# Cross attention on one core: the queries of two row tiles made by one set of split products, and what is moved for it

## The chip, the core and the metric

One core of a Trainium2 chip runs the whole kernel in one launch. The metric is device time in microseconds. The kernel before has a median of 1503.9 us over three runs (1502.83 to 1505.37). TensorE (PE), VectorE (DVE), ScalarE (ACT), GpSimd (POOL) and SyncE (SP, which only issues DMAs here) each work through a queue of their own, and meet at semaphores. TensorE writes to PSUM, which has eight banks of 512 fp32 columns; DVE and ACT read it.

## The reference, cut to what matters

x is 64 sequences of 32 rows with 512 channels; the context is 64 sequences of 257 rows with 256 channels. Three layers follow each other, each with a residual: cross attention, a small self attention, and a mixture of experts (8 experts, 2 per row). The change is in the first:

```
Q = layernorm(x) @ Wq.T                         # 2048 x 512, 16 heads of 32
K, V = split(ctx @ Wkv.T)                       # 64 x 257 x 512 each
attn = softmax(Q K.T * 32**-0.5)                # per sequence and head: 32 x 257
x = x + (attn @ V) @ Wo.T
```

## The kernel before, in words

The 2048 rows are 16 tiles of 128 rows, that is four sequences each. Cross attention never makes K and V: a tile's queries are multiplied into Wk once (`absorb_k`, which makes `QK`, for all 16 heads), and the scores of a sequence are `QK` times the turned context. The weighted sum is taken over the raw context (`gather_z`) and goes through the value weights afterwards (`values`). So a tile has a part of its own (normalise, turn, project to queries, absorb, values, output projection) and four steps, one for each sequence, numbered s = 4i + j for tile i and sequence j: 64 steps.

A step has a fixed order on PE: `scores(s)` (24 products of 258 columns into the four banks of `bank_s`), `gather_z(s-1)` (12 products of 512 columns into `bank_u`), `turn_z(s+1)` (4 transposes of the next sequence's context), then what the tile's own part puts into this step, then `turn_p(s)` (8 transposes of the normalised probabilities into two banks of `bank_s`). In between DVE takes the maxima of the scores (L696), ACT the exponentials (L596), DVE the reciprocals and the division `Pr` (L703 to L708); then DVE subtracts the low part of the next `QK` (L633, `qk_lo`) and of the next turned context (L628, `z_lo`), for which ACT has made the high parts (L558 `qk_hi`, L541 `z_hi`). `scores(s+1)` waits for `z_lo(s+1)` (semaphore `v_T`). After `turn_p`, ACT and DVE copy and split the turned probabilities (L564, L641), which free the two banks for the next scores.

Numbers go as a high and a low part in fp32r: `product` (L49) issues three matmuls for each pair of operands (high by high, low by high, high by low; L52, L53, L54). The query projection is the exception: `project_q` (L394) multiplies plain fp32, `WqT` by the turned rows `xnT`, 128 columns a matmul, one tile at a time; its 16 matmuls of a tile show as 32 records.

What the tile's own part puts into the four steps of tile i: j=0: `turn_last`, `last_values` and `values` of tile i-1 (their result goes over `bank_o`); j=1: `project_o(i-1)` (12 products of 512 columns); j=2: `turn_x(i+2)` (L147, 4 transposes into `bank_o`, copied to `xnT` by ACT, L152) and the first half of `project_q(i+2)`; j=3: its second half. In j=0 and j=2 two `absorb_k` of the next tile (32 small matmuls, L404) stand ahead of them; ACT copies their result to `QK` (L551, two copies of 128x1024), and `turn_p` waits for that copy, because both use `bank_s`. `bank_o` is one bank: turned rows, queries, values and output projection take it in turn, each waiting until the one before has been read.

The order is written out by hand in `tile(i, u, first, last, more)` of each engine. `by_pair` runs tiles in pairs (u = 0 is the even tile, u = 1 the odd); the first and the last pair are written out, the six between are a loop. `more` is false in the last pair. Before it stands a setup block which loads and turns the weights, ending at a barrier, and then a short head which makes the first tiles' queries. The loads of the self attention's weights are issued by SP in the first tile (`weights.load`), and ACT waits for them behind the last step.

Of the kernel before, what the change touches and what calls it, by code (L numbers as in the profile page):

```python
# [23 lines left out]
P = 128  # L24
# [60 lines left out]
def cross_attention(nc, x_in, ctx_in, Wq, Wkv, Wo, x_res, ident, vlast_dram, spare,  # L85
# [21 lines left out]
    with ExitStack() as ctx:  # L107
# [6 lines left out]
        WqT = sb("WqT", [P, KC, C])  # L114
# [11 lines left out]
        key_of = sb("key_of", [P, HD], F32R)  # L126
        xn, xnT = spare_x[:, 0, :], spare_x[:, 1, :].rearrange("p (k q) -> p k q", q=P)
# [9 lines left out]
        pe_X, a_X = sem("pe_X"), sem("a_X")  # L137
# [12 lines left out]
        def x_out(act, i):  # L150
            act.wait_ge(pe_X, i + 1)
            act.copy(xnT.rearrange("p k q -> p (k q)"), bank_o[:]).then_inc(a_X, 1)  # L152

        def rows_of(i):


            return x_res[:, i % n_tile if isinstance(i, int) else i, :]
# [26 lines left out]
        with ExitStack() as setup:  # L184
# [12 lines left out]
            masked = setup.enter_context(nc.semaphore("w_masked"))  # L197
            own_key = sbs("own_key", [P, HD])
# [13 lines left out]
            for k in range(KC):  # L212
                jobs.append((0, [raw_q[:, o, k * P:(k + 1) * P] for o in range(KC)], (WqT[:, k, :], None), P))

            with nc.Block() as block:
# [26 lines left out]
                def _(pe):  # L242
# [4 lines left out]
                    for n, (load, blocks, _dst, width) in enumerate(jobs):  # L247
# [10 lines left out]
                        mm.then_inc(turned, 1)  # L258
                        if n == n_values - 1:
                            turn_x(pe, 0)  # L260

                @block.scalar
                def _(act):
                    for n, (_load, blocks, (hi, _lo), width) in enumerate(jobs):
                        act.wait_ge(turned, n + 1)
                        act.copy(hi, ring[n % 6][:, 0:len(blocks) * width]).then_inc(hi_done, 1)
                        if n == n_values - 1:
                            x_out(act, 0)

                @block.vector  # L270
                def _(dve):
# [3 lines left out]
                    for n, (_load, blocks, (hi, lo), width) in enumerate(jobs[:n_split]):  # L275
# [3 lines left out]
                    dve.tensor_reduce(own_key[:], ident[:].rearrange("p (h t) -> p t h", t=HD), AX_X, ALU.add  # L279
                                      ).then_inc(masked, 1)  # L280
                    dve.tensor_reduce(head_mask[:], ident[:].rearrange("p (h t) -> p h t", t=HD), AX_X, ALU.add
                                      ).then_inc(masked, 1)
                    for j in range(BT):
                        dve.tensor_reduce(row_mask[:].rearrange("p (m j) -> p m j", j=BT)[:, :, j],
                                          ident[:].rearrange("p (b j m) -> p j m b", j=BT, m=NQ)[:, j], AX_X, ALU.add
                                          ).then_inc(masked, 1)
                    dve.wait_ge(masked, 2 + BT)
                    dve.tensor_copy(key_of[:], own_key[:]).then_inc(masked, 1)
# [7 lines left out]
        QK = [sb(f"QK{u}", [P, KL, NH, P]) for u in range(2)]  # L296
# [42 lines left out]
        def step_of(i, u, j, more):  # L339

            if j % 2 == 0 and (more or u == 0):
                return 1 - u, j, 2 * (i + 1) + 2, BT * i + NQ + j + 2
            return None

        with nc.Block() as block:
            @block.sync
            def _(sp):
# [9 lines left out]
                def tile(i, u, first, last, more):  # L359
# [13 lines left out]
                    if first:  # L373
                        weights.load(sp)
                by_pair(sp, tile)

            @block.tensor
            def _(pe):
# [9 lines left out]
                def project_q(i, half, wait_first=True):  # L388
                    pe.wait_ge(a_X, i + 1)
                    if half == 1 and wait_first:  # L390
                        pe.wait_ge(a_Q, 2 * i + 1)
# [81 lines left out]
                project_q(0, 1, False)  # L473
                turn_z(0, 0, 0)
                pe.wait_ge(a_Q, 2)
                turn_x(pe, 1)
                absorb_k(Qp[0], 0)
                absorb_k(Qp[0], 1)
                project_q(1, 0)
# [4 lines left out]
                project_q(1, 1, False)  # L484
# [4 lines left out]
                pe.wait_ge(d_QK, NQ)  # L489

                def tile(i, u, first, last, more):
                    for j in range(BT):
# [3 lines left out]
                        scores(s, some)  # L496
                        if j == 0 and not first:
                            pe.wait_ge(a_Q, 2 * min(i + 2, n_tile) if isinstance(i, int) else 2 * i + 4)
# [39 lines left out]
            def _(act):  # L538
# [4 lines left out]
                def q_out(i, slot, halves):  # L543
                    act.wait_ge(pe_Q, 2 * i + max(halves) + 1)
# [1878 lines left out]
```

## Time and profile before

The profiled execution took 1500.6 us, 3.3 us less than the median; its span is 1498.8 us.

| | |
|---|---|
| median of three runs | 1503.9 us |
| profiled execution, its span | 1500.6 us, 1498.8 us |
| setup block | 0 to 19.1 us |
| cross attention, its 64 steps and their tail | 32.4 to 688 us |
| self attention, routing and experts | from 688 us |
| PE, DVE, ACT, POOL busy over the span | 96%, 73%, 54%, 36% |
| granted TensorE clock, mean | 0.988 of 2.4 GHz |

In a timeline row the first number is the start in us from the span's start, the second the length; a merged row has a count. In brackets stands how long the engine was idle before it and who released it. The ends of matmul records are modelled, so that consecutive records overlap; the distance between two starts is the time that PE spent.

### The profile page before, as it was taken

The page shows a single profiled execution, that of the slowest core. Times are in us where ns is not written, and L with a number is a line of the kernel's source. Part 1 is how long each engine was busy: PE and PEld are TensorE (multiplying, and loading weights), DVE is VectorE, ACT ScalarE, POOL GpSimd, SP SyncE. Part 2 cuts the span into 40 slices and gives each one's busy share as a digit, 9 for nine tenths or more (in the row PEclk, how much of TensorE's full clock was granted, in tenths as well). Part 3 has the DMA queues.
Part 4 walks back from the last instruction along what each step waited for, and adds up shares of the span by engine and source line. Part 5 has one row for each costly group of instructions (what it writes and reads, how often), then busy time and mean ns, then how long its engine had stood idle before and what let it go on. Part 6 is the DMA issues. An engine that isn't in the chain of part 4 may idle for free. (4 is left out here: it accounts for less than half of the span.)

```text
span 1498.8 us, 39481 instructions
## 1 busy us (share of the span) xinstructions
PE 1436.7 (96%) x14944; PEld 1284.1 (86%) x14944; DVE 1087.7 (73%) x1941; ACT 807.3 (54%) x1525; POOL 544.1 (36%) x814
## 2 busy tenths in 40 slices
PE   7999999999999999998899998799999999999998
PEld 6888888888888888876788787688999999999997
DVE  3677777777677776775567686797887878787885
ACT  4666666666666666654333434345555555555452
POOL 1222222222222222234866877453332333334232
PEclk9999999999999999999999999799999999999999
DMA  6301101100001100100001104179877878787871
GB/s 238 126 26 30 30 22 28 28 23 27 28 22 28 28 28 22 30 9 1 31 31 38 38 31 156 59 216 317 270 262 256 274 252 268 261 279 244 289 255 46
DMA packets 130733, 174.10 MB, mean 116 GB/s; under 512 B 16953, under 2 KB 89337, under 8 KB 130626
## 3 DMA queue, kind: packets, MB, share of 16 engines
q1 hardware_dynamic: 120242, 145.56, 30.1%
q0 software_dynamic: 10384, 27.05, 5.0%
q8 instruction: 74, 1.21, 0.3%
q14 instruction: 33, 0.27, 0.1%
HBM read 157.18 MB, written 19.06 MB: 118 GB/s over the span
## 5 line engine op out<-in xcount | busy, mean ns | idle before, releaser
L2215 DVE TENSOR_TENSOR split<-raw,split 128x1024 fp32r<-128x1024 f32 x204 | 242.3, 1220 | 6.6 <-ACT split L2155 4.0
L52 PE MATMUL bank<-split_xT,split 128*128 128x256 f32 x768 | 217.1, 283 | 0.4
L54 PE MATMUL bank<-split_xT,split 128*128 128x256 f32 x768 | 216.2, 282 | 0.0
L53 PE MATMUL bank<-split_xT,split 128*128 128x256 f32 x768 | 216.1, 281 | 0.0
L2155 ACT CAST split<-raw 128x1024 fp32r<-128x1024 f32 x202 | 203.2, 1048 | 5.9 <-DMA raw<-in_L_ffn_W_dram 4.0
L596 ACT ACTIVATE Pr<-xa_s,nmax 128x257 f32<-128x257 f32 x256 | 118.7, 473 | 125.1 <-DVE nmax L696 125.1
L2175 ACT ACTIVATE sl<-bank 128x256 f32<-128x256 f32 x115 | 44.2, 384 | 241.8 <-PE bank L54 232.8
L52 PE MATMUL xa_s<-split,split 128*128 128x258 f32 x512 | 150.6, 294 | 1.9 <-DVE split L628 1.9
L52 PEld LDWEIGHTS bank<-split_xT,split 128*128 128x128 f32 x768 | 145.5, 189 | 6.6 <-issue 2.5
L53 PEld LDWEIGHTS bank<-split_xT,split 128*128 128x128 f32 x768 | 145.6, 190 | 3.2
L53 PE MATMUL xa_s<-split,split 128*128 128x258 f32 x512 | 145.8, 285 | 0.0
L54 PEld LDWEIGHTS bank<-split_xT,split 128*128 128x128 f32 x768 | 145.4, 189 | 0.0
L54 PE MATMUL xa_s<-split,split 128*128 128x258 f32 x512 | 145.3, 284 | 0.0
L641 DVE TENSOR_TENSOR split<-xa_s,split 128x512 fp32r<-128x512 f32 x128 | 82.6, 686 | 81.4 <-ACT split L564 80.2
L2299 POOL TENSOR_TENSOR e_carrier<-count 128x1 f32<-128x1 f32 x84 | 27.2, 324 | 310.2 <-DMA of_row<-slot_val 106.2
L748 POOL TENSOR_TENSOR xa_carrier<-mhalf 128x1 f32<-128x1 f32 x64 | 12.6, 197 | 285.2 <-DVE split L633 280.6
L696 DVE TENSOR_REDUCE nmax<-xa_s 128x2 f32<-128x514 f32 x128 | 87.9, 690 | 33.2 <-PE xa_s L54 32.3
L52 PE MATMUL xa_u<-split,split_xT 128*128 128x512 f32 x256 | 102.3, 400 | 0.8 <-issue 0.8
L52 PE MATMUL bank<-split,a_hi 128*128 128x512 f32 x234 | 96.3, 411 | 7.0 <-DVE a_lo L2274 6.9
L52 PEld LDWEIGHTS xa_s<-split,split 128*128 128x128 f32 x512 | 98.1, 192 | 3.6 <-DVE split L628 2.6
L53 PE MATMUL xa_u<-split,split_xT 128*128 128x512 f32 x256 | 101.0, 395 | 0.0
L54 PE MATMUL xa_u<-split,split_xT 128*128 128x512 f32 x256 | 100.9, 394 | 0.0
(314 smaller groups left out, 3918.5 us busy)
## 6 DMA issues: line engine op xcount, KB each, us to landing
raw<-in_L_ffn_W_dram SPq DMA_DIRECT2D x207, 512.0 KB
raw<-in_ctx_dram SPq DMA_DIRECT2D x64, 256.0 KB, 2.6
out_dram<-x_res SPq DMA_DIRECT2D x16, 256.0 KB
xs<-xn SPq DMA_DIRECT2D x16, 256.0 KB
x_res<-in_x_dram SPq DMA_DIRECT2D x1, 3584.0 KB, 19.0
VL<-v_last_rows SPq DMA_DIRECT2D x128, 2.0 KB, 1.5
raw_o<-in_L_xattn_Wo_dram SPq DMA_DIRECT2D x1, 1024.0 KB, 6.5
raw_q<-in_L_xattn_Wq_dram SPq DMA_DIRECT2D x1, 1024.0 KB, 9.6
```

Of the source, the lines that this page charges most:

```text
L52: pe.matmul(out, lh, rh, start=start, stop=False)
L53: pe.matmul(out, ll, rh, start=False, stop=False)
L54: return pe.matmul(out, lh, rl, start=False, stop=stop)
L596: act.activation(Pr[:, m, 0:NK], bank_s[:, m, 0:NK], ACT.Exp, bias=nmax[:, m:m + 1], scale=1.0, accum_out=rsum[:, m:m + 1]).then_inc(a_E, 1)
L641: dve.tensor_tensor(PT_lo[:, c, :], bank_pt[c], PT_hi[:, c, :].bitcast(F32), ALU.subtract).then_inc(v_PT, 1)
L696: dve.tensor_reduce(nmax[:, 2 * h:2 * h + 2], bank_s[:, 2 * h:2 * h + 2, 0:NK], AX_X, ALU.max, negate=True).then_inc(v_mx, 1)
L748: pool.tensor_tensor(carrier[:], mhalf[:], mhalf[:], ALU.add)
L2155: aW.done(act.copy(hi, raw), f"p{c}{q}")
L2175: aM.done(act.activation(sl[:, j % 2, :], bank_hg[j % 2][:, 0:ROWS], ACT.Silu), f"{pos}s{j}")
L2215: vW.done(dve.tensor_tensor(lo, raw, hi.bitcast(F32), ALU.subtract), f"p{c}{q}")
L2299: pool.tensor_tensor(carrier[:], count[:, 0:1], count[:, 0:1], ALU.add).then_inc(carried, 1)
```

## The change

Only cross attention and its buffers change.

1. `project_q(i, half)` now makes the queries of tiles i and i+1 together, for even i. Operands are split: `WqT_hi`, `WqT_lo`, and `xT_hi`, `xT_lo` which hold the turned rows of two tiles side by side, 256 columns. A half is two blocks of 128 output channels by four of input channels by three matmuls: 24 matmuls of 256 columns, in j=2 and j=3 of the even tile; the odd tile has none. `q_out` writes a half for both tiles with one ACT instruction of 512 columns.
2. `x_out` makes two ACT copies of the turned rows (the plain one stays, and one into `xT_hi`), and a new `x_lo` on DVE subtracts into `xT_lo` (semaphore `v_X`).
3. The rows of tile i+3 are turned in tile i. In the even tile that is in j=2, straight behind the scores, ahead of `gather_z`; its `x_out` stands ahead of `qk_hi` on ACT, its `x_lo` ahead of `qk_lo` on DVE, and `normalise` has moved to the end of j=1. In the odd tile it is in j=3, ahead of `turn_z`; `x_out` stands there ahead of `z_hi`, `x_lo` behind `z_lo`. Tile 2 is turned in the second step of tile 0. `turn_last` in j=0 waits for `a_X`, `v_X` in even tiles and for `a_Q` in odd ones.
4. The odd tile's `project_o(i-1)`, and its `add_residual`, stand in j=2 instead of j=1.
5. Setup: the rows of tiles 0 and 1 are both turned and split there, `WqT` is split (four more DVE subtractions), and the masks (seven small DVE instructions) move behind the barrier. In the head one `project_q(0, half)` of 24 products stands for each half, the second behind the first pair of `absorb_k`.
6. The second `QK` buffer now lies over the places of the self attention's `wq` and `wo`. These two loads (1 MB each) are issued behind the last `qk_lo` (`v_QK`) instead of in the first tile; the others stay.

```diff
-        WqT = sb("WqT", [P, KC, C])
+        WqT_hi, WqT_lo = sb("WqT_hi", [P, KC, C], F32R), sb("WqT_lo", [P, KC, C], F32R)
+        xT_hi, xT_lo = sb("xT_hi", [P, KC, 2 * P], F32R), sb("xT_lo", [P, KC, 2 * P], F32R)
...
-        def x_out(act, i):
+        def x_out(act, i, slot):
             act.wait_ge(pe_X, i + 1)
-            act.copy(xnT.rearrange("p k q -> p (k q)"), bank_o[:]).then_inc(a_X, 1)
+            act.copy(xnT.rearrange("p k q -> p (k q)"), bank_o[:])
+            act.copy(xT_hi[:, :, slot * P:(slot + 1) * P], bank_o[:].rearrange("p (k q) -> p k q", q=P)).then_inc(a_X, 1)
+
+        def x_lo(dve, i, slot):
+            at = slice(slot * P, (slot + 1) * P)
+            dve.wait_ge(a_X, i + 1)
+            dve.tensor_tensor(xT_lo[:, :, at], bank_o[:].rearrange("p (k q) -> p k q", q=P), xT_hi[:, :, at].bitcast(F32),
+                              ALU.subtract).then_inc(v_X, 1)
...
+                        if n == 1:
+                            turn_x(pe, 0)
                         if n == n_values - 1:
-                            turn_x(pe, 0)
+                            pe.wait_ge(v_X, 1)
+                            turn_x(pe, 1)
+                    warm(8)
...
+                    low(0)
+                    low(1)
                     statistics(dve, 1)
+                    x_lo(dve, 0, 0)
+                    low(2)
                     normalise(dve, 1)
-                    dve.wait_ge(lo_done, n_split)
-                    dve.wait_ge(masked, 3 + BT)
+                    for n in range(3, n_split):
+                        low(n)
+                    x_lo(dve, 1, 1)
+                    for n in range(n_values, len(jobs)):
+                        low(n)
...
-        QK = [sb(f"QK{u}", [P, KL, NH, P]) for u in range(2)]
+        QK = [sb("QK0", [P, KL, NH, P]), later_13.rearrange("p k (h t) -> p k h t", t=P)]
...
                     if first:
-                        weights.load(sp)
+                        weights.load(sp, False)
                 by_pair(sp, tile)
+                sp.wait_ge(v_QK, s_end)
+                weights.load(sp, True)
...
-                    for m in range(2 * half, 2 * half + 2):
+                    for m in range(2):
+                        w = slice((2 * half + m) * P, (2 * half + m + 1) * P)
                         for k in range(KC):
-                            mm = pe.matmul(bank_o[:, m * P:(m + 1) * P], WqT[:, k, m * P:(m + 1) * P], xnT[:, k, :],
-                                           start=(k == 0), stop=(k == KC - 1))
+                            mm = product(pe, bank_o[:, m * 2 * P:(m + 1) * 2 * P], (WqT_hi[:, k, w], WqT_lo[:, k, w]),
+                                         (xT_hi[:, k, :], xT_lo[:, k, :]), k == 0, k == KC - 1)
...
                         scores(s, some)
+                        if j == 2 and more and u == 0:
+                            turn_ahead(i, first)
...
-                        if j == 2 and not last:
-                            need(pe, v_OP, i)
-                            turn_x(pe, i + 2)
+                        if first and j == 1:
+                            turn_x(pe, 2)
+                        if j == 3 and more and u == 1:
+                            turn_ahead(i, False)
...
-                        if j == 1 and not first:
+                        if j == 1 + u and not first:
                             project_o(i - 1)
-                        if j == 2 and more:
-                            project_q(i + 2, 0)
-                        if j == 3 and more:
-                            project_q(i + 2, 1)
+                        if j >= 2 and more and u == 0:
+                            project_q(i + 2, j - 2)
...
+                        if j == 2 and more and u == 0:
+                            x_out(act, i + 3, 1)
                         if not (last and j == BT - 1):
                             t = u if j < BT - 1 else 1 - u
                             qk_hi(s + 1, t, (j + 1) % BT, BT * i + (BT if j < BT - 1 else 2 * BT))
-                        if j == 2 and not last:
-                            x_out(act, i + 2)
+                        if first and j == 1:
+                            x_out(act, 2, 0)
+                        if j == 3 and more and u == 1:
+                            x_out(act, i + 3, 0)
...
+                        if j == 2 and more and u == 0:
+                            x_lo(dve, i + 3, 1)
                         if not (last and j == BT - 1):
                             qk_lo(s + 1, u if j < BT - 1 else 1 - u, (j + 1) % BT)
                             z_lo(s + 1)
-                        if j == 1:
-                            if first:
-                                dve.wait_ge(x_rest, 16)
-                            statistics(dve, i + 2)
+                        if first and j == 0:
+                            dve.wait_ge(x_rest, 16)
+                            statistics(dve, 2)
+                        if first and j == 1:
+                            x_lo(dve, 2, 0)
+                        if j == 1 and not last:
+                            statistics(dve, i + 3)
+                        if j == 3 and more and u == 1:
+                            x_lo(dve, i + 3, 0)
```

## Rows read from the trace of the kernel before

**Rows 1.** Busy us by stretch: length, PE, PEld, DVE, ACT, POOL; PEclk, DMA share, GB/s.

```profile
38.00:50.00 12.00, 9.90 (x66) 9.11 (x59) 6.20 (x10) 6.68 (x15) 2.33 (x5) 0.72 0.75 264
315.50:395.50 80.00, 79.54 (x740) 71.33 (x739) 57.43 (x100) 52.14 (x118) 18.88 (x43) 1.00 0.09 27
597.00:688.00 91.00, 80.36 (x708) 69.26 (x707) 65.52 (x110) 51.85 (x115) 21.15 (x44) 1.00 0.06 16
```

**Rows 2.** PE's timeline, steps 29 to 32 (start us, us, engine, line, operation).

```profile
325.69 0.37 PE L52 MATMUL xa_s<-split,split 128*128 128x258 f32 x1
...
331.80 0.48 PE L52 MATMUL xa_o<-split,split_xT 128*128 128x512 f32 x1
...
334.68 1.03 PE L412 MATMUL xa_s<-ident,Pr 128*128 128x128 f32 x8
...
335.47 0.37 PE L52 MATMUL xa_s<-split,split 128*128 128x258 f32 x1
...
341.23 0.60 PE L147 MATMUL xa_o<-ident,xg 128*128 128x128 f32 x4
341.67 0.60 PE L385 MATMUL xa_z<-ident,raw 128*128 128x128 f32 x4
...
343.30 2.05 PE L394 MATMUL xa_o<-xg,WqT 128*128 128x128 f32 x16
...
346.26 0.36 PE L52 MATMUL xa_s<-split,split 128*128 128x258 f32 x1
...
352.46 1.95 PE L394 MATMUL xa_o<-xg,WqT 128*128 128x128 f32 x16
...
354.25 1.04 PE L412 MATMUL xa_s<-ident,Pr 128*128 128x128 f32 x8
...
355.04 0.37 PE L52 MATMUL xa_s<-split,split 128*128 128x258 f32 x1
```

**Rows 3.** PE's timeline, the end of step 58, step 59, the start of step 60.

```profile
628.31 1.09 PE L412 MATMUL xa_s<-ident,Pr 128*128 128x128 f32 x8 [2.10 <-ACT QK L551]
629.16 0.36 PE L52 MATMUL xa_s<-split,split 128*128 128x258 f32 x1
...
637.40 0.39 PE L52 MATMUL xa_s<-split,split 128*128 128x258 f32 x1 [0.64 <-DVE split L628]
```

**Rows 4.** ACT's timeline, step 30 (odd tile's third step).

```profile
341.87 0.58 ACT L152 COPY xg<-xa_o 128x512 f32<-128x512 f32 x1 [0.54 <-PE xa_o L147]
342.35 0.59 ACT L541 CAST split<-xa_z 128x512 fp32r<-128x512 f32 x1
```

**Rows 5.** ACT's timeline, step 59.

```profile
635.55 0.59 ACT L541 CAST split<-xa_z 128x512 fp32r<-128x512 f32 x1 [0.55 <-PE xa_z L385]
```

**Rows 6.** DVE's timeline, step 59.

```profile
636.66 0.68 DVE L628 TENSOR_TENSOR split<-xa_z,split 128x512 fp32r<-128x512 f32 x1
```

**Rows 7.** DVE's timeline, step 1.

```profile
52.22 0.68 DVE L160 BATCH_NORM_STATS2 st<-x_res 128x6 f32<-128x512 f32 x1
```

**Rows 8.** PE's timeline in the experts: 48 products of 256 columns from 1200.28 on.

```profile
1200.28 0.28 PE L52 MATMUL bank<-split_xT,split 128*128 128x256 f32 x1
...
1205.93 0.39 PE L52 MATMUL bank<-split,a_hi 128*128 128x512 f32 x1
```

**Rows 9.** All engines' timeline, the end of the setup block.

```profile
17.34 1.09 ACT L266 COPY WqT<-xa_u 128x512 f32<-128x512 f32 x2
...
19.10 1.13 PE L394 MATMUL xa_o<-xg,WqT 128*128 128x128 f32 x8 [1.45 <-PEq L215]
```

**Rows 10.** DVE's timeline, step 62.

```profile
663.97 1.22 DVE L633 TENSOR_TENSOR split<-QK,split 128x1024 fp32r<-128x1024 f32 x1
```

**Rows 11.** ACT's timeline, behind the last step.

```profile
674.02 2.86 ACT L833 CAST split<-raw 128x2048 fp32r<-128x2048 f32 x2
679.01 1.01 ACT L572 COPY U<-xa_u 128x1024 f32<-128x1024 f32 x1 [2.13 <-PE xa_u L54]
```

**Rows 12.** DMA issues: what, queue, kind, count, KB, us to landing.

```profile
raw<-in_L_attn_wo_dram SPq DMA_DIRECT2D x1, 1024.0 KB, 9.9
```

More of the change, by code:

```diff
@@ L136, in cross_attention @@
         x_first, x_rest = sem("x_first"), sem("x_rest")
-        pe_X, a_X = sem("pe_X"), sem("a_X")
+        pe_X, a_X, v_X = sem("pe_X"), sem("a_X"), sem("v_X")
         z_in = [spare.w13[:, j // 2, 2 * (j % 2):2 * (j % 2) + 2, :] for j in range(BT)]
@@ L212, in cross_attention @@
             for k in range(KC):
-                jobs.append((0, [raw_q[:, o, k * P:(k + 1) * P] for o in range(KC)], (WqT[:, k, :], None), P))
+                jobs.append((0, [raw_q[:, o, k * P:(k + 1) * P] for o in range(KC)], (WqT_hi[:, k, :], WqT_lo[:, k, :]), P))
             with nc.Block() as block:
@@ L274, in _, with low @@
                     normalise(dve, 0)
-                    for n, (_load, blocks, (hi, lo), width) in enumerate(jobs[:n_split]):
+                    def low(n):
+                        _load, blocks, (hi, lo), width = jobs[n]
                         dve.wait_ge(hi_done, n + 1)
@@ L386, in turn_z, with project_q @@
                     mm.then_inc(pe_T, 1)
[L388 to L391, printed above, removed]
-                    for m in range(2 * half, 2 * half + 2):
+                def project_q(i, half):
+                    if half == 0:
+                        pe.wait_ge(a_X, i + 2)
+                        pe.wait_ge(v_X, i + 2)
+                    else:
+                        pe.wait_ge(a_Q, 2 * i + 2)
+                    for m in range(2):
+                        w = slice((2 * half + m) * P, (2 * half + m + 1) * P)
                         for k in range(KC):
-                            mm = pe.matmul(bank_o[:, m * P:(m + 1) * P], WqT[:, k, m * P:(m + 1) * P], xnT[:, k, :],
-                                           start=(k == 0), stop=(k == KC - 1))
+                            mm = product(pe, bank_o[:, m * 2 * P:(m + 1) * 2 * P], (WqT_hi[:, k, w], WqT_lo[:, k, w]),
+                                         (xT_hi[:, k, :], xT_lo[:, k, :]), k == 0, k == KC - 1)
                     mm.then_inc(pe_Q, 1)
@@ L472, in _ @@
                 project_q(0, 0)
[L473 removed]
                 turn_z(0, 0, 0)
                 pe.wait_ge(a_Q, 2)
[L476 removed]
                 absorb_k(Qp[0], 0)
                 absorb_k(Qp[0], 1)
[L479 removed]
+                project_q(0, 1)
+                pe.wait_ge(a_Q, 4)
                 pe.wait_ge(a_QK, 2)
@@ L489, in _, with turn_ahead @@
                 pe.wait_ge(d_QK, NQ)
+                def turn_ahead(i, first):
+                    need(pe, v_OP, i)
+                    if first:
+                        pe.wait_ge(a_X, 3)
+                        pe.wait_ge(v_X, 3)
+                    turn_x(pe, i + 3)
                 def tile(i, u, first, last, more):
@@ L496, in tile @@
                         scores(s, some)
+                        if j == 2 and more and u == 0:
+                            turn_ahead(i, first)
                         if j == 0 and not first:
-                            pe.wait_ge(a_Q, 2 * min(i + 2, n_tile) if isinstance(i, int) else 2 * i + 4)
+                            if u == 1:
+                                pe.wait_ge(a_Q, min(2 * i + 6, 2 * n_tile) if isinstance(i, int) else 2 * i + 6)
+                            else:
+                                pe.wait_ge(a_X, i + 3)
+                                pe.wait_ge(v_X, i + 3)
                             need(pe, v_OP, i - 1)
@@ L613, in tile @@
                         pt_hi(s)
-                        if j >= 2 and more:
-                            q_out(i + 2, u, (j - 2,))
+                        if j >= 2 and more and u == 0:
+                            q_out(i + 2, j - 2)
                 by_pair(act, tile)
@@ L699, in tile @@
                             last_rows(i - 1)
-                        if j == 2:
-                            normalise(dve, i + 2)
+                        if first and j == 1:
+                            normalise(dve, 2)
+                        if j == 2 and u == 1 and not last:
+                            normalise(dve, i + 3)
                         dve.wait_ge(a_E, 4 * s + 4)
@@ L725, in tile @@
                             last_weights(i)
-                        if j == 1 and not first:
+                        if j == 1 and u == 0:
+                            normalise(dve, i + 3)
+                        if j == 1 + u and not first:
                             add_residual(i - 1)
@@ L761, in tile @@
                         split_z(s, j, i)
-                        if j == 1:
-                            rstd_of(pool, i + 2)
+                        if first and j == 0:
+                            rstd_of(pool, 2)
+                        if j == 1 and not last:
+                            rstd_of(pool, i + 3)
                 by_pair(pool, tile)
@@ L838, in low, with load @@
         dve.tensor_tensor(lo, raw, hi.bitcast(F32), ALU.subtract).then_inc(self.lo_done, 1)
-    def load(self, sp):
-        for dst, src in self.loads:
+    def load(self, sp, late):
+        for dst, src in self.loads[0:2] if late else self.loads[2:]:
             sp.dma_start(dst, src).then_inc(self.got, 16)
@@ L2370, in perceiver_block @@
         x_zero = ctx.enter_context(nc.semaphore("xs_zeroed"))
-        slots = [WeightSlot(nc, ctx, c, C, 2) for c in range(W1.shape[2] // (2 * P))]
+        raw = sb("raw", [P, W1.shape[2] // (2 * P), 6 * C])
+        slots = [WeightSlot(nc, ctx, raw, c, C, 2) for c in range(W1.shape[2] // (2 * P))]
         xg = sb("xg", [P, 2, C])
@@ L2391, in perceiver_block @@
             cross_attention(nc, x.rearrange("b t c -> (b t) c"), ctx_512, xWq, xWkv, xWo, x_res, ident,
-                            v_last, slots[0], xg, held, weights, clear_slots)
+                            v_last, slots[0], raw[:, 1:3, 0:4 * C], xg, held, weights, clear_slots)
             banks = Banks(nc, ctx)
```

61 lines of the change are left out of this document (33 added, 28 removed).

## The prediction

> **What bounds the kernel now.** I read the busy time by stretch first. In two undisturbed tiles of cross attention PE is busy 79.5 of 80 us and DVE 57, ACT 52 [rows 1]: it looks as if PE's work alone set the time. Then PE's timeline, step by step, for what stands between two scores. Step 29 of an odd tile (its j=1) runs from 325.69 to 335.47, 9.78 us; step 30 (j=2) to 346.26, 10.79; step 31 (j=3) to 355.04, 8.78 [rows 2]. The reader is to see that a step has a second limit, the chain of the softmax: scores, maxima, exponentials, division, then `qk_lo` and `z_lo` on DVE, and only then the next scores. The trace shows it bare in step 59, an even tile of the last pair, which has no query projection: PE has only scores, gather, 4 transposes and `turn_p`, waits 0.64 us for `z_lo`, and the step takes 637.40 - 629.16 = 8.24 us [rows 3]. So 8.24 us is a floor of every step, however little PE does in it. Step 58 in front of it, a j=2 without projection, shows the third limit: `turn_p` waited 2.10 us for ACT's copy of `QK` [rows 3]. There a projection of 1.79 us costs nothing at all.
>
> **The change part by part**, for a pair of tiles with `more` true. I take each step by its own limit.
>
> *The price of a half.* Before, 16 records of fp32 take 354.25 - 352.46 = 1.79 us [rows 2]; a pair has four such halves, 7.16 us. After, a half is 24 products of 256 columns. 48 of that shape take 1205.93 - 1200.28 = 5.65 us in the experts [rows 8], so 24 take 2.82, and a pair has two, 5.64 us. PE does 1.5 us less work in a pair. Scores are products of 258 columns and no faster, so I see no reason for another figure than 2.82 by over 0.1.
>
> *Even tile, j=2.* `turn_x` moves ahead of the gather and costs the same 341.67 - 341.23 = 0.44 us [rows 2]. I checked that it does not wait: `normalise` and the residual add are done before the scores end. The projection starts at 343.30; before, it would have ended at 345.09, and with `turn_p`, 355.04 - 354.25 = 0.79, the next scores could have started at 345.88; they start at 346.26 [rows 2], 0.38 later, held by the copy of `QK`. After, 343.30 + 2.82 + 0.79 = 346.91: 0.65 us longer. *Even tile, j=3.* Bound by PE on both sides: 2.82 for 1.79, 1.03 us longer. Even tile together: +1.68. The other moved pieces there (two copies on ACT instead of one, a subtraction on DVE ahead of `qk_lo`, normalise a step earlier) push the next step's high and low parts back by about 1 us, beneath a PE that is late by more; if that cover were gone they would cost that 1 us.
>
> *Odd tile, j=1.* `project_o`, 334.68 - 331.80 = 2.88 us [rows 2], leaves. PE alone would give 6.9 us for the step; the floor gives 8.24. So 9.78 becomes 8.24, -1.54. DVE still has the statistics here, behind `z_lo` and ahead of the low part of the probabilities, which the third block of the next scores waits for. The statistics (0.68 us for the first of them [rows 7]) were beneath `project_o`. That wait costs between 0 and 0.7 us; I take 0.2, since the first two blocks of scores still cover most of it. Sum -1.34.
>
> *Odd tile, j=2.* `turn_x` leaves (0.44) and `project_o` comes for the projection: 343.30 - 0.44 + 2.88 + 0.79 = 346.53 against 346.26 [rows 2], +0.27. PE now covers the copy of `QK`.
>
> *Odd tile, j=3.* The projection (1.79) leaves, `turn_x` (0.44) comes, so PE is short again and the chain sets the step. But this time the chain has become longer, because `x_out` with its two copies stands ahead of `z_hi` on ACT. In step 59 `z_hi` starts at 635.55, 6.39 us behind the scores' start, and `z_lo` at 636.66, 7.50 [rows 3, 5, 6]. In step 30 the copy `x_out` starts at 341.87 and `z_hi` at 342.35: a copy costs 0.48 [rows 4]. Turned rows are ready when turned context was, since they are turned first; so `z_hi` starts at 6.39 + 2 x 0.48 = 7.35 and ends 0.59 later, at 7.94. `z_lo` goes from 7.50 to 7.98, 0.48 later, and the step from 8.24 to 8.72. Before it took 8.78: -0.06. This is where the change should have had its second gain, and does not. Bounds: 8.24 (the copies hidden, -0.54) and 9.4 (the extra `x_lo` on DVE, 0.68 as `z_lo` [rows 6], also in front of the next scores, +0.6). I take 8.72. The j=0 steps keep their order; their wait on `a_X`, `v_X` or `a_Q` is over by then; 0 to +0.1 each, taken 0.
>
> *Pair:* 1.68 - 1.34 + 0.27 - 0.06 = +0.55 us. Seven pairs have `more` true: +3.9.
>
> *First and last pair.* Tile 0's j=1 never had an output projection, so it has no 1.5 us to win, and now it carries `turn_x`, both copies and `x_lo` in its chain: 0.48 + 0.68, +1.2. Tile 14 loses its `turn_x` in j=2, ahead of an `absorb_k` whose copy sets that step: -0.44. Tile 15 only swaps j=1 and j=2: 0.
>
> *Setup and head.* Before, ACT's last two copies start at 17.34 and PE leaves the barrier at 19.10 [rows 9]. ACT gets three copies more (two pairs of `x_out` for one single), at 0.48 [rows 4] 1.5 us; behind its last copy DVE must now subtract once more, 0.68 [rows 6]; and the turn of tile 1 stands between the value weights and `Wq`, behind a chain over DVE and POOL, for which I add 0.2. Sum +2.4. From below, ACT's copies alone with some of them in idle time, 1.0; from above, all six new DVE subtractions exposed (6 x 0.68) and the copies too, 5.6. The head is an alternation of projection, query copy and `absorb_k` on both sides; I get the same length within 0.2.
>
> *Late weight loads.* The last `qk_lo` ends at 665.19 [rows 10]. `wo`, the last of seven loads issued together, landed 9.9 us behind its issue [rows 12]; with 0.5 for a second issue that would be 675.6. ACT starts on the weights at 674.02, and had 2.13 us idle behind them [rows 11], so it may start as late as 676.15. Cost 0; at most 2 us if the two megabytes take as much again.
>
> *Sum:* 3.9 + 1.2 - 0.4 + 2.4 = +7.1 us. On the profiled execution, 1500.6, that gives 1507.7; its span would be 1505.9. The median of before is 3.3 us above that execution, so the median to expect is 1503.9 + 7.1 = 1511.0.
>
> **A rule to weigh.** PE is busy 79.5 of 80 us [rows 1]. The Trainium skill (Perfetto Trace Analysis, section Identifying the Most-Contended Engine) says that the engine with the highest occupancy is the one to relieve first, though it warns against taking the matmul busy share as TensorE's measure. By the rule a change that takes work off PE is a gain, 1491 as worked out below; by the rows of step 59 it is not, 1511. The gain is the first rival.
>
> **The rivals.**
>
> *PE's work decides after all (faster).* If the short steps ran as fast as PE can, j=1 would take 6.9 us and j=3 8.78 - 1.79 + 0.44 = 7.43. The pair would be 1.68 + (6.9 - 9.78) + 0.27 + (7.43 - 8.78) = -2.3 us; seven pairs -16, with 3.2 for the ends -13: 1491. For it: PE's busy share. Against it: 8.24 us in step 59, with DVE named as the releaser. It decides only if the chain from scores to `z_lo` became 1 us shorter in these steps, and nothing in the change shortens it. Chance 0.08.
>
> *The bubbles are smaller than I price them (no change).* Copies hidden in j=3 (-0.48), statistics hidden (-0.2), a half at 2.7 instead of 2.82 (-0.24): the pair gives -0.4, seven -2.6, the ends -0.4 + 0.7, setup +1.0 to +2.4: 0 us around, 1504. For it: 8.24 has been seen. Against it: both copies come ahead of `z_hi` in ACT's order. Chance 0.15.
>
> *The clock.* From 38 to 50 us, behind two waits in tile 0, the granted clock had a mean of 0.72 [rows 1]: 12 x 0.28 = 3.4 us lost. Setup and head now have more idle PE, so that such a stretch may come twice (1514.4), chance 0.11; if each odd tile brought one it would be 7 x 3.4 = 24 us (1535), chance 0.03. Against the latter: in the tail of the last pair PE waited 2.10 and 0.64 us close together [rows 3], and the clock was 1.00 from 597 to 688 [rows 1]. The low stretch may also vanish, 3.4 us back, which is in the range.
>
> **How the numbers follow.** Forecast 0.60; the three rivals 0.37; 0.03 for what I have not seen. Range: from 1504.5 (half of the no-change case in it) to 1516 (pair at +1.2 with a setup of 4, or the forecast with a second low stretch). A measurement of this kernel tells about 0.2%, 3 us, from no change. Faster by over that: 0.08, and 0.02 from unseen things, 0.10. Within: 0.10 of the second rival and 0.05 of the forecast's own low edge, 0.15. Slower: 0.75.
>
> **What would show it.** In the changed kernel's PE timeline the pair's eight steps should read 11.0, 9.8, 11.4, 9.8 and 11.0, 8.2, 11.3, 8.7. In the odd tile's second and fourth step PE should wait for `z_lo` before the scores, by 0.6 and 1.1 us or so, and `z_hi` in the fourth should stand behind two `x_out` copies. The barrier should be left near 21.5. The first self attention matmul should come 7 us later than 688. Wrong it would be if the odd tile's j=1 took under 8 us, if j=3 of the odd tile took 8.2, or if the halves' 24 products took other than 2.8 us.

## The result and the profile after

| | before | after |
|---|---|---|
| median of the runs beside each other | 1503.4 us (4 runs) | 1512.8 us (4 runs) |
| ratio, 95% interval | | 1.0064 [1.0052, 1.0077] |
| profiled execution, its span | 1500.6, 1498.8 us | 1512.9, 1511.1 us |
| PE busy over the span | 1436.7 us | 1430.7 us |
| first scores at | 32.4 us | 35.6 us |
| a pair of tiles, steady | 80.8 us | 81.7 us |
| last step's scores at | 665.8 us | 674.6 us |
| first product of the self attention at | 687.9 us | 699.0 us |

The kernel became 9.5 us slower, while PE became 6 us less busy. The forecast was 1511.0 us, 7.1 us slower; the direction and the way it comes about were right, and the size was too small.

The page of the changed kernel, two of its first lines, against 1436.7 us of PE before:

```profile
span 1511.1 us, 39279 instructions
...
PE 1430.7 (95%) x14832; PEld 1273.4 (84%) x14832; DVE 1097.9 (73%) x1962; ACT 814.4 (54%) x1528; POOL 547.7 (36%) x814
```

In PE's timeline of the changed kernel these are the steps 34 to 39, the second half of an even tile and the whole odd one. A step runs from one `xa_s<-split,split` row that opens the scores to the next. In brackets, `PEq` stands for PE's own sequencer:

```profile
380.90 0.36 PE L52 MATMUL xa_s<-split,split 128*128 128x258 f32 x1
...
388.76 0.39 PE L52 MATMUL xa_o<-xT_hi,WqT_hi 128*128 128x256 f32 x1
...
391.72 1.04 PE L435 MATMUL xa_s<-ident,Pr 128*128 128x128 f32 x8
...
392.51 0.36 PE L52 MATMUL xa_s<-split,split 128*128 128x258 f32 x1
...
402.37 0.36 PE L52 MATMUL xa_s<-split,split 128*128 128x258 f32 x1
...
413.40 0.36 PE L52 MATMUL xa_s<-split,split 128*128 128x258 f32 x1
...
419.91 1.09 PE L435 MATMUL xa_s<-ident,Pr 128*128 128x128 f32 x8 [0.15 <-DVE Pr L757]
...
421.64 0.39 PE L52 MATMUL xa_s<-split,split 128*128 128x258 f32 x1 [0.64 <-DVE split L665]
...
424.84 0.40 PE L52 MATMUL xa_u<-split,split_xT 128*128 128x512 f32 x1
...
432.97 0.36 PE L52 MATMUL xa_s<-split,split 128*128 128x258 f32 x1
...
441.70 0.39 PE L52 MATMUL xa_s<-split,split 128*128 128x258 f32 x1 [1.07 <-DVE split L665]
```

What to read from it, with the time before from [rows 2] in brackets:

- even tile, third step, 380.90 to 392.51: 11.61 us (10.79); fourth step: 9.86 (8.78);
- odd tile, second step, 413.40 to 421.64: 8.24 us (9.78), with PE waiting 0.64 for `z_lo` exactly as in [rows 3];
- odd tile, third step: 11.33 us (10.79). Its scores alone, 421.64 to 424.84, take 3.20 us, where those of the other steps take 2.96;
- odd tile, fourth step, 432.97 to 441.70: 8.73 us (8.78), where PE waits 1.07.

The 24 products of a half take 391.72 - 388.76 = 2.96 us.

ACT and then DVE in that last step, where [rows 4, 5] show one copy or none ahead of `z_hi`:

```profile
439.36 0.59 ACT L155 COPY xg<-xa_o 128x512 f32<-128x512 f32 x1 [0.54 <-PE xa_o L150]
439.85 0.59 ACT L156 CAST xT_hi<-xa_o 128x512 fp32r<-128x512 f32 x1
440.32 0.60 ACT L574 CAST split<-xa_z 128x512 fp32r<-128x512 f32 x1
```

```profile
440.96 0.69 DVE L665 TENSOR_TENSOR split<-xa_z,split 128x512 fp32r<-128x512 f32 x1 [0.39 <-ACT split L574]
```

Two copies of the turned rows (`xg` and `xT_hi`) stand ahead of `z_hi`, which starts 7.35 us behind the scores' start (forecast 7.35), and DVE, idle for 0.39 us, starts `z_lo` at 7.99 (forecast 7.98).

The setup block's end in all engines (before, PE left it at 19.10, [rows 9]):

```profile
19.80 1.28 DVE L293 TENSOR_TENSOR WqT_lo<-xa_u,WqT_hi 128x512 fp32r<-128x512 f32 x2
...
21.60 0.37 DVE L718 TENSOR_REDUCE own_key<-ident 128x32 f32<-128x128 f32 x1 [0.53 <-PEq L223]
...
21.75 0.36 PE L52 MATMUL xa_o<-xT_hi,WqT_hi 128*128 128x256 f32 x1 [1.37 <-PEq L223]
```

Busy time of a steady pair and of the tail, columns as in [rows 1]. Over the pair PE has 2.1 us idle, against 0.5 in 80 us before; and the granted clock is 0.95 from 600 to 720:

```profile
360.05:441.70 81.65, 79.53 (x728) 70.75 (x728) 58.93 (x103) 53.72 (x119) 19.76 (x43) 1.00 0.10 26
600.00:720.00 120.00, 106.58 (x942) 91.21 (x941) 78.91 (x131) 66.48 (x140) 36.58 (x72) 0.95 0.10 30
```

**Where the 12.3 us of span between the two profiled executions went.** Two causes are mixed in it: the changed steps, and stretches of low clock that the two executions had in different places.

- *Setup and head:* the first scores come 3.3 us later.
- *First pair:* 79.4 us for 80.3. But before, the clock was low in its first two steps, which took 9.85 and 10.16 us. With the clock at 1.00 such steps take 9.07, as after, and 8.24, as step 59 and as e1 below. Without these 2.7 us the pair is 1.8 longer.
- *Six steady pairs:* 6 x 0.87 = +5.2.
- *Last pair:* +1.2. Now the clock was low here, in two steps that took 10.91 and 9.30 us; in s3 below, with the same work in them, they take 10.42 and 8.24. That cost 1.6, so without the clock the last pair is 0.4 shorter.
- *Tail up to the self attention:* +2.4, the clock again: 12 gather products took 5.25 us there for 2.87.
- *Behind it:* +1.1.

What does not hang on the clock is 3.3 + 1.8 + 5.2 - 0.4 = 9.9 us, next to 9.5 from the medians.

### The profile page after: what moved, and what is told of

Same layout as the page of the kernel before. It is cut to its first block and busy times, and to the rows that moved or that the text cites. A ratio compares the mean times of both kernels' runs of the same rounds, so it can differ in the third digit from the quotient of the medians.

```text
span 1511.1 us, 39279 instructions
## 1 busy us (share of the span) xinstructions
PE 1430.7 (95%) x14832; PEld 1273.4 (84%) x14832; DVE 1097.9 (73%) x1962; ACT 814.4 (54%) x1528; POOL 547.7 (36%) x814
## 5 line engine op out<-in xcount | busy, mean ns | idle before, releaser
L52 PE MATMUL xa_u<-split,split_xT 128*128 128x512 f32 x256 | 104.0, 406 | 0.7 <-issue 0.7
L54 PE MATMUL xa_u<-split,split_xT 128*128 128x512 f32 x256 | 101.9, 398 | 0.0
L53 PE MATMUL xa_u<-split,split_xT 128*128 128x512 f32 x256 | 101.8, 398 | 0.0
```

The source lines that it names most:

```text
L52: pe.matmul(out, lh, rh, start=start, stop=False)
L53: pe.matmul(out, ll, rh, start=False, stop=False)
L54: return pe.matmul(out, lh, rl, start=False, stop=stop)
```

## The experiments

Each ran beside the kernel before, and times are given against that. Its median was 1501.0 us beside e1, e2, e3 and b1, and 1504.1 beside e5, b2, f1 and s1; s2, s3 and s4 are single runs, beside one run of 1502.7. The changed kernel was not run again beside them, so distances from it go over the kernel before. e1, e2, e3, e5, f1 and the four s runs are edits of the changed kernel, b1 and b2 of the kernel before.

**The floor of a short step.** First, work was taken from PE in the kernel before, three quarters of one half of each projection, so that these kernels compute other queries. `n_k=1` takes one of the four blocks of input channels.

```diff
-                            project_q(i + 2, 1)
+                            project_q(i + 2, 1, n_k=1)
```

> The kernel before with three quarters of the second half of each tile's query projection left out (the fourth step keeps 4 of 16 records), so PE has 1.34 us less to do in 14 steps. Theory (floor of the chain): the fourth step goes from 8.78 to 8.24 and no lower, 14 x 0.54 = 7.6 us faster than the kernel before. Rival (PE's work decides): 14 x 1.34 = 18.8 us faster.

Measured 0.9965 [0.9950, 0.9980], 5.3 us faster, where 7.6 was expected; the step itself is as expected in all 14 places. PE's timeline, the step that held the shortened half:

```profile
421.59 0.36 PE L52 MATMUL xa_s<-split,split 128*128 128x258 f32 x1
...
427.79 0.61 PE L394 MATMUL xa_o<-xg,WqT 128*128 128x128 f32 x4
428.24 1.04 PE L412 MATMUL xa_s<-ident,Pr 128*128 128x128 f32 x8
...
429.84 0.39 PE L52 MATMUL xa_s<-split,split 128*128 128x258 f32 x1 [0.57 <-DVE split L628]
```

The step takes 8.25 us, with 0.57 us of idle PE in front of the next scores: 1.34 us of work gone, 0.53 gained. In the other half it buys nothing:

```diff
-                            project_q(i + 2, 0)
+                            project_q(i + 2, 0, n_k=1)
```

> The kernel before with three quarters of the first half of each tile's query projection left out (the third step keeps 4 of 16 records), so PE has 1.34 us less to do in 14 steps. Theory (in that step the copy of QK decides): the third step stays at 10.8, no difference from the kernel before. Rival (PE's work decides): 14 x 1.34 = 18.8 us faster.

Measured 1.0002 [0.9985, 1.0020]. The step stays at 10.79, and the row of `turn_p` names the third limit, ACT's copy of `QK`:

```profile
415.12 0.37 PE L52 MATMUL xa_s<-split,split 128*128 128x258 f32 x1
...
422.95 0.71 PE L394 MATMUL xa_o<-xg,WqT 128*128 128x128 f32 x4
425.06 1.09 PE L412 MATMUL xa_s<-ident,Pr 128*128 128x128 f32 x8 [1.41 <-ACT QK L551]
425.91 0.36 PE L52 MATMUL xa_s<-split,split 128*128 128x258 f32 x1
```

Then the chain itself was shortened, and PE's work left as it was. This is the changed kernel with one copy of the turned rows (e1, below), in which DVE divides only half of the probabilities, so that its numbers are wrong.

```diff
-                        dve.tensor_tensor(Pr[:, :, 0:LAST], Pr[:, :, 0:LAST], ...
+                        dve.tensor_tensor(Pr[:, :, 0:P], Pr[:, :, 0:P], ...
```

> e1_one_copy with the division of the probabilities done for half of the columns, so that this DVE instruction in the chain takes 0.6 instead of 1.2 us; the other half goes on undivided. Theory (the floor is the chain through DVE up to z_lo): the steps at 8.24 us fall to 7.7, all steps bound by PE stay: 17 or 18 such steps, 10 us under e1_one_copy, 3 to 4 us under the kernel before. Rival (the short steps are held by something else, such as banks or POOL): nothing changes.

Measured 0.9974 [0.9960, 0.9987], 3.9 us under the kernel before, and so 10.5 under e1. The odd tile's second step went to 7.75 us as expected in all seven pairs, its fourth did not: it stayed at 8.25. The DVE timeline of such a fourth step says why:

```profile
435.73 0.69 DVE L756 TENSOR_TENSOR Pr<-Pr,rinv 128x512 f32<-128x512 f32 x1
436.37 1.23 DVE L669 TENSOR_TENSOR split<-QK,split 128x1024 fp32r<-128x1024 f32 x1
437.99 0.69 DVE L664 TENSOR_TENSOR split<-xa_z,split 128x512 fp32r<-128x512 f32 x1 [0.39 <-ACT split L573]
```

DVE was through with `qk_lo` and idle for 0.39 us until ACT's `z_hi` came. So the floor has two branches that end at the same `z_lo`: DVE's division and `qk_lo`, and, where a copy stands ahead of it, ACT's `z_hi`. The expectation had only the first. That the total came out as expected is luck in part: with the last pair, which has two more such steps, nine steps became 0.5 us shorter and one 0.2. That is 4.6 us, where 17 or 18 steps and 10 us were expected, and what made up the rest is not shown.

**The second copy.**

```diff
-            act.copy(xnT.rearrange("p k q -> p (k q)"), bank_o[:])
             act.copy(xT_hi[:, :, slot * P:(slot + 1) * P], ...
```

> The changed kernel with one ACT copy of the turned rows (into xT_hi) where it had two; the plain rows of the last one, which the next layer reads, are put together again by POOL behind the last step. PE's work is the same. Theory (in the odd tile's fourth step the chain scores, exponentials, z_hi, z_lo decides, and the second copy lengthens it): that step goes from 8.73 to 8.25 us in seven pairs, -3.4, tile 0's second step -0.5, setup -0.5: 4.4 us under the changed kernel, so 5 us over the one before. Rival (PE's amount of work decides): no difference from the changed kernel, 9.5 us over the one before.

Measured 1.0047 [1.0034, 1.0061], 6.6 us over the kernel before: 4.4 was expected of the copy, and by the medians it is about 3. The steps show it more directly: the odd tile's fourth is 8.25 us for 8.73 in all seven pairs, tile 0's second 8.24 for 8.74, the first scores come at 35.06 for 35.62, 4.4 us together. In the even tile, where PE's work sets the step, the copy costs nothing: the third step is 11.62 with one and 11.61 with two.

```profile
430.01 0.36 PE L52 MATMUL xa_s<-split,split 128*128 128x258 f32 x1
...
435.77 0.60 PE L150 MATMUL xa_o<-ident,xg 128*128 128x128 f32 x4
...
438.26 0.39 PE L52 MATMUL xa_s<-split,split 128*128 128x258 f32 x1 [0.59 <-DVE split L664]
```

**Where the odd tile's output projection stands.** This undoes one part of the change, for the output projection on PE and, by the same edit, for the residual add on DVE.

```diff
-                        if j == 1 + u and not first:
+                        if j == 1 and not first:
```

> The changed kernel with the odd tile's output projection and residual add back in its second batch. PE's work is the same. Theory (each step has a floor of 8.24 us, and one with absorb_k of 10.4): the second step goes from 8.24 to 9.79, the third from 11.33 to 10.41, the pair +0.6, seven pairs +4.4: 14 us over the kernel before. Rival (PE's work decides): unchanged at 9.5 us over it.

Measured 1.0108 [1.0090, 1.0125], 16 to 17 us over the kernel before where 14 were expected. The steps read 9.79, 10.35, 8.73 in the odd tile, 0.6 us more a pair. PE waits 2.05 us for the copy of `QK` again:

```profile
428.68 0.36 PE L52 MATMUL xa_s<-split,split 128*128 128x258 f32 x1
...
438.19 1.09 PE L435 MATMUL xa_s<-ident,Pr 128*128 128x128 f32 x8 [2.05 <-ACT QK L584]
439.04 0.36 PE L52 MATMUL xa_s<-split,split 128*128 128x258 f32 x1
```

Part of the rest is the clock: the profiled execution of this kernel had a mean of 0.982, and steps of 10.24 and 10.27 in two places where others have 8.73. So this part of the change, taken by itself, is a gain of 4 us by the steps, and of about 7 by the medians. On top of e1, the same products were then cut in two:

```diff
-                        if j == 1 + u and not first:
+                        if j == 1 and u == 0 and not first:
                             project_o(i - 1)
+                        if j == 1 and u == 1:
+                            project_o(i - 1, 0, NQ // 2)
+                        if j == 2 and u == 1:
+                            project_o(i - 1, NQ // 2, NQ)
```

> The changed kernel with one ACT copy as in e1_one_copy, and with the odd tile's output projection cut in two: six products in its second step, six in its third. Theory (floors): second step 8.35 (PE and chain about equal), third 10.41 (down from 11.33, held by the copy of QK), fourth 8.25: the pair 80.4 for 81.7, seven pairs -9.2, last pair -1.3, tile 0 and setup -1: 11 us under the changed kernel, so 1 to 2 us under the one before. Rival (PE's work decides): 9.5 us over the one before.

Measured 1.0020 [1.0008, 1.0032], 3.4 us over the kernel before, not 1 to 2 under it. The steps are as expected: 8.39, 10.45, 8.33, a pair 80.5. In its profiled execution the last step's scores start at 666.5 us, 0.7 behind the kernel before; from there to the self attention it takes 3.5 us longer, with a mean granted clock of 0.94 from 600 to 720 us. So the order did what was expected of it in the steps. The expectation left out what a low stretch in the tail costs; how many of the other executions had one is not known.

**All steps at or above their floor.** With step costs known, the projection was cut into three parts and laid where PE was idle. One copy, as in e1, stays.

```diff
+                        if j == 1 and u == 1 and more:
+                            project_q(i + 1, 3, 1)
+                        if j == 2 and u == 1 and more:
+                            pe.wait_ge(a_Q, 2 * i + 6)
+                            project_o(i - 1)
...
+                        if j == 2 and more and u == 0:
+                            project_q(i + 2, 0, 2)
+                        if j == 3 and more and u == 0:
+                            project_q(i + 2, 2, 1)
```

> One ACT copy as in e1_one_copy, and the two tiles' projection in three parts: 24 products in the even tile's third step, 12 in its fourth, 12 in the odd tile's second; the odd tile's output projection stands whole in its third step (only in the last tile it is cut in two, as in e3_o_split). PE's work is that of the changed kernel. Theory (a step costs the larger of PE's work in it and its floor): the even tile's fourth step goes from 9.85 to 8.4, just over the floor, the odd tile's second from 8.24 to 8.4: the pair 79.9 us, against 81.2 in e1_one_copy and 80.8 before. Seven pairs -9.2 and the last pair -1.3 against e1_one_copy: 3 to 4 us faster than the kernel before. Rival (PE's amount of work decides): same as e1_one_copy, 6 to 7 us over the one before.

Measured 0.9960 [0.9948, 0.9973]: 1498.3 against 1504.1 us, 5.8 us faster than the kernel before, where 3 to 4 were expected, and so some 15 faster than the changed one. Of these 15 some 4 are e1's copy, by its steps; the order is worth the rest. PE's timeline, the even tile's fourth step and the odd tile's four:

```profile
386.67 0.36 PE L52 MATMUL xa_s<-split,split 128*128 128x258 f32 x1
...
395.07 0.36 PE L52 MATMUL xa_s<-split,split 128*128 128x258 f32 x1
...
406.12 0.36 PE L52 MATMUL xa_s<-split,split 128*128 128x258 f32 x1
...
414.53 0.36 PE L52 MATMUL xa_s<-split,split 128*128 128x258 f32 x1
...
425.68 0.36 PE L52 MATMUL xa_s<-split,split 128*128 128x258 f32 x1
...
433.93 0.39 PE L52 MATMUL xa_s<-split,split 128*128 128x258 f32 x1 [0.58 <-DVE split L683]
```

They are 8.40, 11.05, 8.41, 11.15 and 8.25 us; only in the last does PE wait for `z_lo`. A pair takes 79.7 us, against 81.2 in e1, which has the same products.

**The setup.** What ends the setup block of the changed kernel? All four s runs leave out DVE's four subtractions for `WqT_lo` and set it to zero. In s1 POOL does so, ahead of its other work for tile 1:

> The changed kernel with the four subtractions that make WqT_lo left out; POOL sets it to zero, so that PE has the same products. Theory (DVE's queue ends the setup block): the barrier comes 1.1 us earlier, where ACT's last copy of WqT ends, so 8.4 us over the kernel before instead of 9.5, and the first scores at 34.5 instead of 35.6. Rival (PE, which waits for the second tile's rows, or ACT ends the setup): the barrier stays at 21.7.

Measured 1.0069 [1.0048, 1.0091], 8.9 us over the kernel before. The first query product comes at 21.55 and the first scores at 35.40, where 20.6 and 34.5 were expected: a miss. While POOL's memset ran, DVE's first `normalise` took 3.09 us instead of 1.34 (last section), so that PE turned tile 0 at 13.26 instead of 11.90 and tile 1 at 16.94 instead of 16.22. PE's warming products then ended last, at 21.1. So the question was put again with the memset behind POOL's work for tile 1:

> As s1_no_low_wq (no subtractions for WqT_lo in the setup, POOL sets it to zero), but POOL does so behind the second tile's rstd, so that the second tile's rows come no later than in the changed kernel. Theory (DVE's queue ended the setup block of the changed kernel, with PE's last 8 warming products the next limit, 0.7 us ahead): the first query product comes at 21.0 to 21.1 instead of 21.75. Rival (the way over the second tile's rows and ACT's copies decides): it stays within 0.2 us of 21.75.

A miss again: 21.92 us (1513.0 us in all, one run). This time the memset met DVE's second `normalise`, and tile 1 was turned at 17.20. With the warming products also gone:

> As s2_low_wq_later, and the 8 warming products behind the turns left out. Theory: ACT's last copy of WqT, ending at 19.9, is what is left: first query product at 20.5 to 20.6. Rival (the warming products were no limit): as s2_low_wq_later. If the warming products keep the clock up, the granted clock of the first 60 us falls below 1.00 here and not in s2_low_wq_later.

22.43 us (1514.3 us in all, one run), a third miss, and inconclusive for the question, since the turns of `Wq` themselves ran slow. The granted clock of the first 60 us had a mean of 0.89, against 0.97 in s2 and 1.00 in the changed kernel. In s4 DVE sets `WqT_lo` to zero itself, at the very start:

```diff
+                    dve.memset(WqT_lo[:].bitcast(F32), 0.0).then_inc(lo_done, 1)
...
-                    for n in range(n_values, len(jobs)):
-                        low(n)
```

> The changed kernel without the four subtractions for WqT_lo; DVE sets it to zero at the very start, before any data has come, so that nothing else moves (s1 and s2 had POOL do it, and that delayed the second tile's rows by 0.7 to 1.0 us). Theory (the barrier follows the last of DVE's low parts of Wq in the changed kernel, at 21.08, by 0.67): PE's warming products, ending at 20.4, are now last, and the first query product comes at 20.9 to 21.1. Rival (DVE's queue did not end the setup): it stays at 21.75.

The first query product comes at 20.77 us, a little earlier than expected, and the first scores at 34.63 for 35.62. All engines' timeline:

```profile
18.37 1.95 PE L253 MATMUL xa_z<-ident 128*128 128x128 f32 x16
...
20.61 0.37 DVE L718 TENSOR_REDUCE own_key<-ident 128x32 f32<-128x128 f32 x1 [1.99 <-PEq L223]
...
20.77 0.36 PE L52 MATMUL xa_o<-xT_hi,WqT_hi 128*128 128x256 f32 x1 [0.45 <-PEq L223]
```

So DVE's queue did end the setup block of the changed kernel; without these subtractions PE's warming products (`xa_z<-ident`, over at 20.3) do, and the block is left 1.0 us earlier. Its time (1515.6, one run) says nothing of this: the clock had a mean of 0.91 over its first 60 us, and the first two steps took 11.21 and 10.39.

## Why the prediction was right, and where it was short

The forecast was right in its mechanism. Its size was short by 2.4 us, through several small terms, and in one place the sum was nearer than its terms.

- *A step costs the larger of PE's work and a floor of 8.24 us.* Shown: by the changed kernel's 8.24 in all seven odd second steps, by b1 (8.25 and no lower) and by f1 (lower when the chain is shorter). The Trainium skill (Perfetto Trace Analysis, Identifying the Most-Contended Engine) says to optimise the engine with the highest occupancy first. It does not say that any work taken off that engine saves time, as the prediction's first rival read it; read so, it has the wrong sign here: PE's busy time fell by 6 us and the kernel took 9.5 more.
- *The first half was hidden beneath the copy of `QK`.* Shown by b2.
- *Odd j=3 gains nothing, because of the two copies.* Forecast 8.72, measured 8.73; with one copy 8.25.
- *Odd j=1 and j=2.* Forecast 8.24 and 11.3, with 0.2 of it for the wait behind the statistics; measured 8.24 and 11.33. The wait can be read: the scores of the odd tile's third step take 3.2 us for 2.96 in all six steady pairs, and 2.96 again in e2, where they start later.
- *The price of a half was too small.* 24 products of 256 columns take 2.96 us, not 2.82, which is one of the prediction's own signs of being wrong. Rows 8 come from the middle of a long row of products, 0.118 us apart; here they are 0.12 apart, and the second of each group comes 0.2 us behind the first. The even tile becomes 1.90 longer instead of 1.68. With 0.07 more in the odd tile's second and third steps and 0.03 in the others, the pair is +0.87 instead of +0.55, and 2 us over six pairs.
- *Setup and head.* Forecast +2.4 with the head unchanged; measured +2.65 at the barrier and +0.6 in the head, where the second query copy waits for all 24 products. That is 0.9 us more. At the barrier DVE ended 1.16 us behind ACT's last copy, not 0.68, since its four subtractions stand behind each other.
- *First pair: the sum was luck.* The prediction puts it at 1.2 above a normal pair, all in tile 0's second step, with 0.68 of it for `x_lo` in front of the next scores. The total is near: 0.9 (1.8 against 0.9). But `x_lo` stands behind `z_lo`, and that step is only 0.5 us longer, which is the copy (e1 takes it away). The rest comes in the step behind it, 12.39 us against 11.62 in a steady pair. There the scores take 3.75 us, because DVE reaches the low part of the probabilities only behind `x_lo` and the statistics; before, with the statistics alone, they took 3.15:

```profile
53.43 0.39 PE L52 MATMUL xa_s<-split,split 128*128 128x258 f32 x1 [1.07 <-DVE split L665]
...
57.18 0.60 PE L150 MATMUL xa_o<-ident,xg 128*128 128x128 f32 x4
```

- *Last pair.* Forecast -0.4, measured -0.4 without the clock.
- *Late weight loads.* Cost 0, as forecast. SP issued them at 672.44 and 672.87, the second landed 7.8 us later, and ACT took up the weights at 682.78 right behind its other work, then waited 4.55 us for the gather.
- *The clock.* It was low in other places than before: not in the first steps, but in the last pair and the tail. The cost differs from execution to execution; up to the self attention the two profiled ones differ by some 1.3 us for it (1.6 + 2.4 - 2.7). With this and the terms above, the first self attention product came 11.2 us later, where the prediction had 7. The rival with a low stretch in each odd tile is ruled out: the clock was 1.00 over the steady pair.

Still open: where a low stretch begins. The changed kernel had its first at the last pair, s3 its own in setup, head and first steps and none in the tail, s4 in head and first steps and none in the tail, e3 and e5 in the first steps and the tail. From the last step's scores to the self attention the executions take 22.0 us or 24.4 us and more by it, so that medians which differ by 2 us should be read with the step table beside them.

## What to carry to other kernels

Before taking work off an engine that is 99% busy, find the least time of each repeated step, in a place where that engine has little to do (a last iteration will do), and put the saved work where the step stands above that floor; a saving in a step at its floor is lost. Here the same products in another order, with one copy taken out of the chain, were worth 15 us. And a copy costs nothing until it stands in the chain in front of what the bottleneck waits for.

## What the runs showed that was not expected

**A DVE instruction stretches beside POOL memsets.** DVE's `normalise` of 128x512 took 0.54 us when POOL did nothing beside it (second tile, changed kernel), and 1.56 in s2, while POOL set 128x2048 to zero. First POOL, then DVE:

```profile
14.97 1.79 POOL L247 MEMSET WqT_lo<- 128x2048 f32 x1
```

```profile
15.49 1.56 DVE L180 TENSOR_SCALAR xg<-x_res,mv,rstd 128x512 f32<-128x512 f32 x1
```

The same shows in s1 for the first tile, POOL's last memset of several and DVE:

```profile
11.12 1.79 POOL L246 MEMSET WqT_lo<- 128x2048 f32 x1
```

```profile
10.11 3.09 DVE L180 TENSOR_SCALAR xg<-x_res,mv,rstd 128x512 f32<-128x512 f32 x1 [0.77 <-POOL rstd L186]
```

Both end 0.29 us behind the end of the memset: 17.05 behind 16.76, and 13.20 behind 12.91. The 1.34 us of this instruction in the other kernels fit too: in the changed kernel it ends at 11.31, and three short memsets at 11.02. So the instruction lasts until POOL's row of memsets is over. Not every DVE instruction does this: in s2 a subtraction with PSUM as one input, which ran beside the memset from 14.97 on, took its usual 0.68.

**A low clock in the setup.** In s3 the 8 transposes of `Wq` took 1.92 us instead of 1.04, behind 2.14 us of idle PE; the granted clock was 0.50 from 18 to 20 us. The warming products that s3 leaves out stand behind these transposes, so their absence is not the cause, and s2 had the same 2.14 us of idle PE with the clock at 1.00. Which of the two a run gets is open.
